# MLP products in halves between the scores, layer 1's queries and keys at the transposed scores, and a tiny exponential behind the last gelu

## What is computed

```python
def full_layer(x, cond, context):                      # layers 0, 2, 3
    sh_sa, sc_sa, g_sa, sh_ff, sc_ff, g_ff = split(silu(cond) @ adaln_w + adaln_b, 6)
    xm = ln(x) * (1 + sc_sa) + sh_sa
    q, k, v = split_heads(xm @ qkv_w + qkv_b)
    x = x + g_sa * (softmax(q @ k.T / 4) @ v @ sa_proj_w + sa_proj_b)
    q = heads(ln(x) @ q_w + q_b)                       # layer 2: ln with gamma and beta
    k, v = heads(context @ kv_w + kv_b)                # layer 3: ln(context)
    x = x + softmax(q @ k.T / 4) @ v @ ca_proj_w + ca_proj_b
    xm = ln(x) * (1 + sc_ff) + sh_ff
    h = gelu(xm @ fc1_w + fc1_b)                       # 256 -> 1024
    return x + g_ff * (h @ fc2_w + fc2_b)              # 1024 -> 256

def layer_1(x, cond, context):                         # adaLN on both sides
    q = (ada_ln(x, cond) @ Wq + bq);  k, v = ada_ln(context, cond) @ Wkv + bkv
    return x + softmax(q @ k.T / 4) @ v @ Wp + bp
```

## Time and profile before

| | before |
|---|---|
| median of the runs | 2684.3 us |
| the profiled execution's own time | 2690.53 us |
| its span on the core | 2688.7 us |
| TensorE busy | 2513.9 us, 93% of the span |
| VectorE busy | 1849.4 us, 69% |
| ScalarE busy | 1253.9 us, 47% |
| GpSimd busy | 454.9 us, 17% |
| granted TensorE clock, mean | 0.975 of full speed |

### The profile page before, as it was taken

How to read it: one execution, slowest core, us unless ns; L and a number is a source line. 1 busy time by engine, 2 the same in 40 slices (tenths; PEclk the granted TensorE clock), 3 DMA queues, 4 the chain that set the end, 5 groups by cost and what they waited for, 6 DMA issues and landing times.

```text
span 2688.7 us, 66128 instructions
## 1 busy us (share of the span) xinstructions
PE 2513.9 (93%) x27522; PEld 1888.4 (70%) x27522; DVE 1849.4 (69%) x3543; ACT 1253.9 (47%) x1759; POOL 454.9 (17%) x461
## 2 busy tenths in 40 slices
PE   6779899999999999999999999999999999999988
PEld 5546677777777777777677777777777777777766
DVE  3466677777777777777776766777777777777742
ACT  0233555444444455555545445454454545445442
POOL 0011211111121111111111111111211121111111
PEclk7688999999999999999999999999999999999999
DMA  5232222222222223232121212122131222313210
GB/s 183 80 97 64 81 76 71 80 81 81 71 71 75 80 71 97 71 103 74 51 75 62 86 51 89 57 89 84 62 114 61 88 71 67 92 55 94 64 40 28
DMA packets 236651, 207.54 MB, mean 77 GB/s; under 512 B 87634, under 2 KB 221972, under 8 KB 236356
## 3 DMA queue, kind: packets, MB, share of 16 engines
q1 hardware_dynamic: 236356, 203.32, 24.1%
HBM read 58.34 MB, written 4.39 MB: 23 GB/s over the span
## 4 chain that ended last, share of the span: by engine, by line
PE 76%; DVE 12%; issue 6%; ACT 5%; DMA 1%; SPq 1%; POOL 0%; POOLq 0%; DVEq 0%; ACTq 0%
PE ring L1237 12%; PE ring L1227 10%; PE ring L1115 10%; PE o_acc L1205 9%; PE score L1153 9%; PE score L1175 7%; PE ring L1217 5%; DVE row_max_F L858 4%; PE ring L1014 4%; DVE row_max_G L858 4%; PE ring L1123 3%; PE ring L1134 2%; PE score L1180 2%; ACT probs L994 2%; PE ring L1137 2%
## 5 line engine op out<-in xcount | busy, mean ns | idle before, releaser
L994 ACT ACTIVATE probs<-score 120x2048 f32<-120x2048 f32 (+1 forms) x320 | 602.1, 1881 | 258.9 <-PE score L1180 249.4
L858 DVE TENSOR_REDUCE row_max_F<-score 128x8 f32<-128x2048 f32 x192 | 438.0, 2281 | 63.7 <-PE score L1153 63.5
L1227 PE MATMUL ring<-x_t_E,w_fc 128*128 128x256 f32 x1536 | 379.3, 391 | 0.0
L1237 PE MATMUL ring<-w_fc,h_t 128*128 128x256 f32 x1536 | 363.0, 388 | 1.0 <-ACT h_t L1005 1.0
L1005 ACT ACTIVATE h_t<-ring,cols 128x256 f32<-128x256 f32 x384 | 161.2, 471 | 423.6 <-PE ring L1227 423.6
L1237 PEld LDWEIGHTS ring<-w_fc,h_t 128*128 128x128 f32 x1536 | 284.7, 191 | 59.4 <-issue 17.8
L1227 PEld LDWEIGHTS ring<-x_t_E,w_fc 128*128 128x128 f32 x1536 | 277.2, 189 | 67.4 <-issue 19.1
L858 DVE TENSOR_REDUCE row_max_G<-score 128x16 f32<-128x1920 f32 x128 | 276.0, 2157 | 51.5 <-PE score L1153 51.5
L880 DVE STREAM_TRANSPOSE o_turned<-o_acc 128x512 f32<-128x512 f32 x224 | 159.5, 712 | 125.5 <-PE o_acc L1205 123.8
L1205 PE MATMUL o_acc<-probs,v_self 128*17 128x256 f32 x3072 | 209.9, 391 | 1.0 <-ACT probs L994 1.0
L1115 PE MATMUL ring<-x_t_P,w_qk 128*128 128x256 f32 x768 | 194.4, 398 | 2.7 <-ACT x_t_P L946 2.5
(11 more groups left out here) (133 smaller groups left out, 3856.1 us busy)
## 6 DMA issues: line engine op xcount, KB each, us to landing
q_G<-q_parts SPq DMA_DIRECT2D x256, 128.0 KB, 2.1
q_F<-q_parts SPq DMA_DIRECT2D x192, 128.0 KB, 2.1
k_F<-k_parts SPq DMA_DIRECT2D x96, 256.0 KB, 2.5
k_F<-k_parts SPq DMA_DIRECT2D x192, 128.0 KB, 2.2
k_G<-k_parts SPq DMA_DIRECT2D x128, 120.0 KB, 2.2
k_G<-k_parts SPq DMA_DIRECT2D x256, 60.0 KB, 1.9
gate_now_P<-gate_rows SPq DMA_DIRECT2D x48, 256.0 KB, 3.7
gate_now_E<-gate_rows SPq DMA_DIRECT2D x48, 256.0 KB, 3.8
```

What stands on the lines that cost most here:

```text
L858: nc.vector.tensor_reduce(dst, src, AX.X, ALU.max).then_inc(row_max_ready[r].sem, 1)
L994: nc.scalar.activation(probs[v % 2][0:keys, :, :], score[0:keys, :].rearrange("p (h q) -> p h q", h=2 * GROUPS), ACT.Exp, scale=SCALE).the ...
L1227: last = mm(ps[:, c % 2 * NT:(c % 2 + 1) * NT], w_fc1[:, k, c * P:(c + 1) * P], x_t[r][:, k, :], start=k == 0, stop=k == KC - 1)
L1237: last = mm(ps[:, 0:D], h_t[:, k, t * P:(t + 1) * P], w_fc2[:, k, :], start=k == 0, stop=k == MC - 1)
```

## The change

Both tables are reordered, F20 is split as F21 was, and ScalarE gets one more instruction in each MLP sample.

**Halves.** F20 becomes F20a and F20b, 4 products each, in one ring bank; nobody may use that bank between the two. In `TURN`, F20a and F20b still stand together, and F21a moves from the last row to the row of G.T1, three rows ahead of F21b. In `WITH_L1` the four halves stand in the rows of 1G.S1, G.S0, G.S1 and F.T0.

**Moves in `TURN`.** R.C goes from F.T1 to G.S0, P.K from G.T0 to F.T1 (where R.LN was), R.LN from F.T1 and e.LN from F.T2 to G.T0, R.Q from G.T1 to F.T2 and R.KV from F.T2 to F.T3.

**Moves in `WITH_L1`.** P.Q and P.K go from rows of the scores (1G.S0, G.S1) to the first transposed scores, 1G.T0 and 1G.T1; 1R.Q and 1R.KV go from F.T0 and F.T1 to F.T1 and G.T0; H1 goes from S1 to S2, P.LN from S2 to S1, A.PR from S3 to 1G.S0, 1R.LN from 1G.S0 to S3, 1R.C from 1G.S1 to 1G.S0, 1B.PR from G.T0 to G.T1 and e.LN from G.T1 to F.T3. R.N goes from behind 1G.S1 to behind G.S0's products, R.A and e.N to G.S1, e.A to 1G.T0.

**Tiny exponential.** Behind the gelus of H3 ScalarE takes the exponential of one column into `fetched`. The table load now stands ahead of it and not ahead of the first exponential of the scores. It waits for its own predecessor alone.

```diff
 F.T0 G.M P.Q R.A R.RES e.N
-F.T1 F.PV0 R.LN R.C e.A
-G.T0 F.PV1 F.O0 P.K p.N
+F.T1 F.PV0 P.K e.A
+G.T0 F.PV1 F.O0 R.LN e.LN p.N
...
-        elif step == "F21b":
+        elif step in ("F20b", "F21b"):
-            here = next(b for br, bm, bs, bn, b in reversed(out) if (br, bm, bs, bn) == (r, m, "F21a", n))
-            assert all(b != here for br, bm, bs, bn, b in out[[e[:4] for e in out].index((r, m, "F21a", n)) + 1:])
+            first_half = [e[:4] for e in out].index((r, m, step[:3] + "a", n))
+            here = out[first_half][4]
+            assert all(e[4] != here for e in out[first_half + 1:])
...
                     last.then_inc(h_ready.sem, 1)
+                    if i == 3:
+                        if self_order[m, n] == 0:
+                            act.wait_ge(const_ready, CONSTS)
+                        else:
+                            act.wait_ge(table_fetched, self_order[m, n])
+                        nc.scalar.activation(fetched[:, :], minus_half[:, 0:1], ACT.Exp).then_inc(table_fetched, 1)
...
-                    if in_ring[here] and step != "F21b":
+                    if in_ring[here] and step not in ("F20b", "F21b"):
                         drained(*in_ring[here])
...
-                    halves = {"F20": range(MC), "F21a": range(MC // 2), "F21b": range(MC // 2, MC)}
-                    for k in halves[step]:
+                    for k in range(MC // 2) if step[3] == "a" else range(MC // 2, MC):
                         last = mm(ps[:, 0:D], h_t[:, k, t * P:(t + 1) * P], w_fc2[:, k, :],
                                   start=k == 0, stop=k == MC - 1)
-                    if step != "F21a":
+                    if step[3] == "b":
                         last.then_inc(f2_psum.sem, 1)
```

More of the change, by code:

```diff
@@ L50 @@
 F.S3 F.X E.H3 A.PR
-G.S0 F.M B.PR E.RES
-G.S1 G.X E.F20 R.N
+G.S0 F.M B.PR R.C E.RES
+G.S1 G.X E.F20a E.F20b R.N
 F.T0 G.M P.Q R.A R.RES e.N
-F.T1 F.PV0 R.LN R.C e.A
-G.T0 F.PV1 F.O0 P.K p.N
-G.T1 G.PV0 G.O0 R.Q p.A c.NC
-F.T2 G.PV1 G.O1 R.KV e.LN c.AC
-F.T3 F.PV2 E.F21a E.F21b
+F.T1 F.PV0 P.K e.A
+G.T0 F.PV1 F.O0 R.LN e.LN p.N
+G.T1 G.PV0 G.O0 E.F21a p.A c.NC
+F.T2 G.PV1 G.O1 R.Q c.AC
+F.T3 F.PV2 R.KV E.F21b
 P.ld c.ld P.gld E.gld P.ST
@@ L62 @@
 F.S0 f.PV3 f.O1 E.H0
-F.S1 E.H1 P.V P.RES
-F.S2 E.H2 P.LN
-F.S3 F.X E.H3 A.PR 1R.RES
-1G.S0 F.M 1R.LN P.Q E.RES
-1G.S1 1G.X B.PR 1R.C R.N
-G.S0 E.F20 1G.M R.A R.RES
-G.S1 G.X P.K
-1G.T0 E.F21a e.N
-1G.T1 1G.PV0 1G.O0 E.F21b G.M e.A
-F.T0 1G.PV1 1G.O1 1R.Q p.N
-F.T1 F.PV0 1R.KV p.A
-G.T0 F.PV1 F.O0 1B.PR
-G.T1 G.PV0 G.O0 R.LN R.C e.LN
-F.T2 G.PV1 G.O1 R.Q 1p.NC 1p.N
-F.T3 F.PV2 R.KV 1p.AC 1p.A
+F.S1 P.V P.LN P.RES
+F.S2 E.H1 E.H2
+F.S3 F.X E.H3 1R.LN 1R.RES
+1G.S0 F.M A.PR 1R.C E.RES
+1G.S1 1G.X B.PR E.F20a
+G.S0 1G.M E.F20b R.N
+G.S1 G.X E.F21a R.A R.RES e.N
+1G.T0 P.Q e.A
+1G.T1 1G.PV0 1G.O0 P.K
+F.T0 1G.PV1 1G.O1 E.F21b G.M p.N
+F.T1 F.PV0 1R.Q p.A
+G.T0 F.PV1 F.O0 1R.KV
+G.T1 G.PV0 G.O0 R.LN R.C 1B.PR 1p.NC 1p.N
+F.T2 G.PV1 G.O1 R.Q 1p.AC
+F.T3 F.PV2 e.LN R.KV 1p.A
 P.ld 1R.ld c.ld P.gld E.gld P.ST
@@ L89 @@
 ROLE = {"p": "P", "f": "F", "c": "R", "e": "E", "1p": "R", "1R": "R", "1G": "G", "1B": "B"}
-RING_STEPS = ("LN", "C", "Q", "K", "V", "KV", "M", "PR", "H0", "H1", "H2", "H3", "F20", "F21a",
+RING_STEPS = ("LN", "C", "Q", "K", "V", "KV", "M", "PR", "H0", "H1", "H2", "H3", "F20a", "F21a",
               "ZT", "ZC", "ZM", "ZG")
@@ L206, in build_program @@
         minus_half = sb("minus_half", [P, TT])
+        fetched = sb("fetched", [P, 1])
         w_raw = sb("w_raw", [P, KC, 2 * D])
@@ L363, in build_program @@
         const_ready = semaphore("const_ready")
+        table_fetched = semaphore("table_fetched")
         ident_zero = semaphore("ident_zero")
@@ L905, in _ @@
                             .then_inc(x_cross_ready.sem, 1)
-                elif step in ("F20", "F21b"):
+                elif step in ("F20b", "F21b"):
                     t = int(step[2])
```

## The result

| | before | after |
|---|---|---|
| median of the runs | 2683.4 us (2679.1 to 2686.1, 4 runs) | 2662.0 us (2661.3 to 2664.5, 4 runs) |
| the profiled execution's own time | 2690.5 us | 2661.3 us |
| its span | 2688.7 us | 2659.5 us |

The ratio is 0.9919, interval 0.9907 to 0.9930: 21.4 us or 0.8% faster. The forecast was 2669.4 us and 14.9 us of gain, with 8 chances in 10 for 2654 to 2682. The median before is that of four runs here, the three of the front and one of 2679.1 us. The run that was profiled before stands 6 to 7 us above its own median, so the spans differ by more (29.2) than the medians.

The account below looks back on a forecast made before the run. TensorE's queue, busy 93%, was taken as the bound. `TURN` turns -19.0, `WITH_L1` turns +4.5, edges +2.6 and end -3 sum to -14.9: from 2684.3 to 2669.4 us, 8 in 10 for 2654 to 2682.

Parts of the forecast that it names:

- Both waits: `TURN` turns: R.LN's wait for x_hat_R (0.68 each) and G.S1's for the row maxima (0.24 each) would go.
- a small one: `TURN` turns: a new wait of 0.2 us at e.LN, since P.K's low part stands ahead of x_hat_E on VectorE.
- the forecast 1.06: `TURN` turns: gain per turn from the two removed waits, 0.92 together, 1.06 us with the covered ends.
- the covered end: TensorE: a wait that goes gives back some 0.07 us beyond its bracket, the pipelined end of the group ahead.
- The two small ones: `WITH_L1` turns: new waits of 0.09 us between S3 and 1G.S0 and of 0.13 us at 1G.T1.
- The third rival: ScalarE stands still behind the early table load for another 1.28 us, delaying 1R.C; about 2684.9 us, no change; chance 0.04.
- Only 13 us in all hang on it: Rival: the load is already hidden in `TURN` turns, so only 13 us depend on moving it; counted in the sum.
- I take -3, between 0 and -5: End of the kernel: G.T0 and its exponential go ahead of R.LN's 3.16 wait, but e.LN is called earlier; -3 us.
- The +1.5 of turns 4 and 5: `WITH_L1` turns with layer 1 only partly there: thin rows cost +1.0 and +0.5 us.
- put at nothing, plus or minus 6: First 240 us, where the clock is not full: thin rows could keep it down or not; 0, plus or minus 6 us.
- layer 1's turns did not gain: Judges the rival that each of 15 `WITH_L1` turns falls to about 61.3, -20 instead of +4.5, 2645 us; chance 0.14.
- the slower rival: VectorE's queue in `WITH_L1` turns: seven waits each 0.3 longer, 2.4 more a turn, +36-17.4, about 2703 us; chance 0.08.

Follow-up runs that it names:

- y11: y10 with x_hat_E (e.A) made ahead of the keys' low part (P.K) in `TURN`; 2612.1 us, ratio 0.9735.
- x1: Kernel before, both tables in the old order, with only the tiny exponential added; 2668.9 us, ratio 0.9946.
- z12: Kernel before with the new `TURN` only ahead of layer 1 and from turn 47 on, old `WITH_L1`, no tiny exponential; 2674.9 us, ratio 0.9966.
- x5: Changed kernel with H1 back ahead of S2 and P.LN back behind S2 in `WITH_L1`; 2650.6 us, ratio 0.9879.
- x6: Changed kernel with layer 1's x_hat (1p.A) moved from ahead of S0's reduction to behind S2's; 2652.9 us, ratio 0.9886.
- x7: Changed kernel with G.M moved from behind F21b to behind F.T1 in `WITH_L1`; 2653.3 us, ratio 0.9890.
- y9: Changed kernel with `WITH_L1` mended: H1 and 1R.A behind S1, G.M behind F.T1, e.A behind F.O0, e.N and R.A re-sorted; 2626.6 us, ratio 0.9787.
- y10: y9 with F20 cut 2 and 6 products, F21 6 and 2, and F21b ahead of 1G.O1; 2616.7 us, ratio 0.9753.
- x3: Kernel before with the new `TURN` and the tiny exponential, `WITH_L1` left old; 2645.2 us, ratio 0.9857.
- x4: Changed kernel without the tiny exponential; 2662.9 us, ratio 0.9922.

## Why the prediction was right, and where it was off

**The `TURN` turns.** Both waits went and a small one came, as laid out. TensorE at G.T0 and what is ahead of it, then VectorE and ScalarE, in the turn from 1620.85; they answer to the earlier trace rows:

```profile
1649.28 1.99 PE L1125 MATMUL ring<-x_t_P,w_qk 128*128 128x256 f32 x8
1651.20 0.50 PE L1185 MATMUL score<-q_G,k_G 32*120 32x256 f32 x8
...
1653.09 0.66 PE L1024 MATMUL ring<-ident,x_hat_R 128*128 128x128 f32 x4
1653.85 0.63 PE L1024 MATMUL ring<-ident,x_hat_E 128*128 128x128 f32 x4
...
1651.31 0.84 ACT L979 ACTIVATE k_parts<-ring,cols 128x256 fp32r<-128x256 f32 x2 [1.04 <-PE ring L1125]
...
1652.18 0.88 DVE L744 SCALAR_TENSOR_TENSOR k_parts<-ring,cols,k_parts 128x256 fp32r<-128x256 f32 x2 [0.94 <-ACT k_parts L979]
1652.97 0.73 DVE L736 TENSOR_SCALAR x_hat_E<-x,mean_var_E,rstd_E 128x256 f32<-128x256 f32 x2
```

The chain copy, low part, x_hat_E is the one that the prediction counted. x_hat_E's transposes start 0.76 behind x_hat_R's. In y11, where x_hat_E is early, it is 0.49 (rows of TensorE):

```profile
1466.40 0.66 PE L1024 MATMUL ring<-ident,x_hat_R 128*128 128x128 f32 x4
1466.89 0.60 PE L1024 MATMUL ring<-ident,x_hat_E 128*128 128x128 f32 x4
```

The wait is therefore 0.27, not 0.2, and it has no bracket, because the modelled end of the group ahead covers it: an empty list of waits doesn't mean that nothing waits. y11 then gave 0.25 a turn for moving e.A.

A regular turn gained 0.61 (47.38 to 46.77) for a forecast of 0.76 (to 46.6). Counted on TensorE from start to start in the two `TURN` turns of the windows (1725.67 before, 1667.62 after), the forecast 1.06 came: 0.76 behind PV0, and at G.S1, which starts 18.82 behind F.S0 in both, R.C fills the 0.30 that was a wait. F21 in two blocks costs 0.09 for 0.1. The term that was mis-sized is the wait at e.LN: the two groups of transposes take 1.31 (0.75 and 0.56) where they took 0.99 (0.46 and 0.53), 0.32 for 0.2. The last 0.03 lies in pieces of 0.01 to 0.02.

The 24 turns together gained 16.3 us for 18.2, and not only 24 x 0.61 = 14.6, because the kernel before has turns of up to 47.73 among them and the kernel after has none. In four of these (47.52 to 47.71) one normalisation of O on VectorE takes 1.23 to 1.42 beside an instruction of GpSimd where the others take 0.42; the last section has the rows. x1 and z12, with the old order in these turns, have one of 48.3 in their place, and the sums agree to 0.4 us. So some 2 us of the gain were in no term of the sum.

**The `WITH_L1` turns.** 62.90 was forecast and 62.90 came. The waits: S1 0.92 (forecast 1.00), S2 0.91 (1.02), G.S1 0.24 (0.29), 1G.T0 0.51 (0.59), G.M 0.52 (0.56), none at S3's row and at 1G.T1. Each bracket is 0.04 to 0.11 smaller than the sum, which contains the covered end that a bracket leaves out. The two small ones, 0.09 and 0.13, have no bracket for the same reason, but their spacings came: S3 to 1G.S0 is 3.15 (851.96 to 855.11) for 3.14, 1G.T0 to 1G.T1 2.96 (870.22 to 873.18). The queue of VectorE behind S0 in the trace after is the one that made the first two; it answers to the earlier trace rows:

```profile
840.64 0.73 DVE L736 TENSOR_SCALAR x_hat_R<-x,mean_var_R,rstd_R 128x256 f32<-128x256 f32 x2
841.28 2.28 DVE L861 TENSOR_REDUCE row_max_F<-score 128x8 f32<-128x2048 f32 x1
843.48 0.70 DVE L883 STREAM_TRANSPOSE o_turned<-o_acc 128x512 f32<-128x512 f32 x1
...
845.33 2.25 DVE L861 TENSOR_REDUCE row_max_F<-score 128x8 f32<-128x2048 f32 x1
```

x5, x6 and x7 show the cause of three of the five, S2, S1 and G.M: one move takes the wait away, or in S1's case the 0.65 of it that were x_hat's. Those of G.S1 and 1G.T0 went in y9 and y10 together with other moves, and no run takes them one by one. The 15 turns cost 4.2 us for 4.5. What the forecast did not separate is that a gain stands against a loss here: 1.07 a turn lost by the order (x3 against after), 0.78 won by the exponential in the old order (x1).

**The tiny exponential.** ScalarE behind the last gelu, and TensorE at 1R.C, which needs x_t_R out of the ring; it answers to the earlier trace rows:

```profile
854.67 0.84 ACT L1008 ACTIVATE h_t<-ring,cols 128x256 f32<-128x256 f32 x2 [1.76 <-PE ring L1237]
855.52 1.28 ACT L1017 ACT_TABLE_LOAD   x1
856.82 0.20 ACT L1017 ACTIVATE fetched<-minus_half 128x1 f32<-128x1 f32 x1
856.93 1.00 ACT L949 ACTIVATE x_t_R<-ring,mods 128x256 f32<-128x256 f32 x2
...
858.15 0.37 PE L1024 MATMUL ring<-ident,x_hat_C 120*128 120x120 f32 x2
```

The load starts right behind the gelu and the exponential 0.02 behind the load's end, though gelu and copies stand around it. x_t_R ends at 857.93, 0.22 ahead of 1R.C, for a forecast of 0.25. The third rival, and with it the 1.38 us of drain of the Trainium skill ("ScalarE: Activation LUTs", "What ACT_TABLE_LOAD costs"), does not hold in this trace: there is no gap for it on either side of the load. "Only 13 us in all hang on it" was right for the old order; 1G.T1's wait would have gone without the exponential too, as x4 shows.

**The ends: the waits came, the clock was not in the sum.** "I take -3, between 0 and -5": it was -6.6 in the trace after and -6.8 in z12, outside those ends. The row of the last cross sample's R.LN shows the forecast mechanism, 1.62 for 3.16 of the earlier trace rows, and e.LN now waits there too:

```profile
2576.49 1.09 PE L1024 MATMUL ring<-ident,x_hat_R 128*128 128x128 f32 x4 [1.62 <-DVE x_hat_R L736]
2579.49 1.08 PE L1024 MATMUL ring<-ident,x_hat_E 128*128 128x128 f32 x4 [1.90 <-DVE x_hat_E L736]
```

A wait of 3.09 for the exponential at G.T1, for which the prediction had no row, went away with it. In the whole tail the brackets of TensorE sum to 14.9 us for 18.4: 3.5 us less, close to the 3 of the forecast. The other 3 us are in TensorE's busy time, at a higher granted clock. The same stretch, from the last `TURN` turn's F.S0 to the end, in the kernel before, in the kernel after and in x3, which has the kernel after's `TURN` and exponential (the clock is the third number from the end):

```profile
2532.05:2688.70 156.65, 133.62 (x1125) 104.41 (x1124) 64.94 (x128) 54.49 (x83) 24.93 (x23) 0.93 0.11 36
...
2509.48:2659.50 150.02, 130.44 (x1125) 102.29 (x1124) 65.05 (x128) 59.47 (x91) 24.93 (x23) 0.96 0.12 40
...
2487.85:2641.60 153.75, 134.74 (x1125) 104.27 (x1124) 65.06 (x128) 59.56 (x91) 24.94 (x23) 0.93 0.13 39
```

At the clock of before the new order gains 2.9 us here. The twelve profiles with the new `TURN` at this place take 149.8 us (clock 0.97) to 153.8 (0.93); the two with the old one take 156.7 and 156.8 (0.93 and 0.92). So the term had its waits right and left the clock of the last turns out, up to 4 us; why the new order mostly gets more of it is open.

The start is similar. The +1.5 of turns 4 and 5 came: 105.9 us (240.81 to 346.71) became 107.4 (228.48 to 335.85). What was put at nothing, plus or minus 6, is turns 0 to 2. They take 155.5 us in the trace of before at a clock of 0.71, 148.0 in x1 with the same table at 0.76, and 143.2 to 145.9 in the twelve with the new `TURN`, at 0.75 to 0.76. So 2 to 5 us are the order's, and 7.5 lie between two profiles of the same table. The medians leave -3 for the start, z12 -2 to -3. How much of this is waits and how much the clock stays open. (By the earlier trace rows the clock is full from the fifth slice on, after some 270 us, and not from the fourth.)

The other rivals: layer 1's turns did not gain, and VectorE's queue was not longer than laid out. (The sum of the slower rival has a slip: without layer 1's turns the other terms are -19.4, not -17.4, which makes it 2701.) All in all -6.5 us against the forecast: +1.9 in `TURN` turns, -0.3 in layer 1's, +0.1 behind them, -3.6 at the end and -4.6 at the start. The two kinds of full turns came out close by the mechanism that was laid out; the 8 us at the two ends are in part the granted clock of the profiled executions, on which no term of the sum had a hold, and the range took them in.

## What to carry to other kernels

In an order with strict queues, price each step moved also by what it covered where it was, and not only by where it goes. The waits of the new `WITH_L1` turns were for work of VectorE whose cover on TensorE had become too short, and the three that were taken away by one move each gave their brackets back. Where a change makes several moves with one result near zero, try the halves apart: here the table without its `WITH_L1` part is 17 us faster than the whole. Ends of a pipeline with few samples in flight deserve a sum of their own: the same moves take 3.5 us of waits out of the last turns here and 0.6 us out of a full one. And where the granted clock is not full, two profiles of the same order can differ by as much, so compare the clocks of a stretch before its length.
